# A cross-attention kernel: the half tile of keys moved to the seventh step of a group, two score buffers that alternate across groups, queries made in three stacked blocks

## What is computed

```
B = 16 batches, 256 queries of width 128, 1601 keys of width 96, 16 heads of width 64
xn  = layernorm(x)
sim = (xn Wq)(ctx Wk)^T / 8         per head, softmax over the 1601 keys
x   = x + softmax(sim)(ctx Wv) Wo + bo
h   = layernorm(x)
x   = x + experts(h) + shared(h)    32 experts, 4 chosen per token
```

## Time and profile before

| | |
|---|---|
| median of three executions | 3226.2 us |
| the profiled execution: its time, its span | 3223.51 us, 3221.7 us |
| PE matmuls busy | 3179.9 us, 99% |
| weight loads, DVE, ACT, POOL busy | 79%, 74%, 63%, 41% |
| mean granted clock of TensorE | 0.997 of 2.4 GHz |
| DMA, mean over the span | 21 GB/s |

### The profile page before, as it was taken

The page is one execution under the profiler, slowest core; times in us unless marked ns, Lnnn a source line. Parts: engine busy times, 40 slices in busy tenths (PEclk is TensorE's granted clock), DMA queues, the critical chain, the costliest instruction groups (busy, mean ns, idle before and its releaser), DMA issues.

```text
span 3221.7 us, 40836 instructions
## 1 busy us (share of the span) xinstructions
PE 3179.9 (99%) x15118; PEld 2534.7 (79%) x15118; DVE 2389.6 (74%) x4882; ACT 2017.8 (63%) x2356; POOL 1333.2 (41%) x894
## 2 busy tenths in 40 slices
PE   7999999999999999999999999999999999999999
PEld 5777777778777777778777777777877778777787
DVE  5777777777777777777777777777777777777766
ACT  4666666666666666666666666666666666676555
POOL 5333443334333343334443344333433334225566
PEclk8999999999999999999999999999999999999999
DMA  2000000000000000000000000000000000105553
GB/s 82 1 17 1 17 1 1 18 1 18 1 18 1 18 1 1 17 1 18 1 18 1 18 1 18 1 1 18 1 18 1 18 1 1 40 3 122 120 129 76
DMA packets 31707, 67.48 MB, mean 21 GB/s; under 512 B 8339, under 2 KB 9620, under 8 KB 31124
## 3 DMA queue, kind: packets, MB, share of 16 engines
q1 hardware_dynamic: 31508, 64.88, 7.8%
HBM read 61.72 MB, written 2.62 MB: 20 GB/s over the span
## 4 chain that ended last, share of the span: by engine, by line
PE 96%; DVE 1%; POOL 1%; issue 1%; ACT 0%; DMA 0%; POOLq 0%; SPq 0%; DVEq 0%; ACTq 0%
PE st L593 12%; PE st L596 12%; PE side L535 11%; PE op L606 11%; PE op L612 11%; PE st L599 11%; PE op L609 11%; PE side L629 3%; PE st L716 2%; PE st L718 2%; PE st L717 2%; PE side L528 1%; PE op L620 1%; PE op L623 1%; PE side L530 1%; PE side L529 1%
## 5 line engine op out<-in xcount | busy, mean ns | idle before, releaser
L473 POOL TENSOR_TENSOR p_lo<-p_full,p_hi 128x1024 fp32r<-128x1024 f32 x320 | 819.7, 2562 | 1753.1 <-ACT p_hi L877 1753.1
L1156 DVE TENSOR_REDUCE m_part<-side 128x1 f32<-128x400 f32 x2016 | 1072.7, 568 | 502.3 <-PE side L535 502.2
L874 ACT ACTIVATE p_full<-st 128x1024 f32<-128x1024 f32 x768 | 788.8, 1027 | 876.8 <-PE st L599 848.5
L877 ACT ACTIVATE p_hi<-st 128x1024 fp32r<-128x1024 f32 x768 | 784.9, 1022 | 0.0
L1139 DVE TENSOR_TENSOR p_lo<-p_full,p_hi 128x1024 fp32r<-128x1024 f32 x448 | 545.5, 1218 | 85.6 <-ACT p_hi L877 85.6
L535 PE MATMUL side<-cT_hi,qT_hi 96*128 96x400 f32 x2016 | 554.5, 346 | 0.0
L593 PE MATMUL st<-qT_hi,cT_hi 97*128 97x512 f32 x1664 | 540.8, 406 | 11.9 <-DMA qT_hi<-m_row 11.1
L596 PE MATMUL st<-qT_lo,cT_hi 96*128 96x512 f32 x1664 | 524.3, 396 | 0.0
L606 PE MATMUL op<-p_hi,v_hi 128*97 128x512 f32 x1536 | 487.6, 398 | 1.6 <-DVE p_lo L1139 1.6
L612 PE MATMUL op<-p_hi,v_lo 128*97 128x512 f32 x1536 | 480.4, 394 | 0.0
L609 PE MATMUL op<-p_lo,v_hi 128*97 128x512 f32 x1536 | 480.4, 394 | 0.0
(11 more groups left out here) (171 smaller groups left out, 3072.1 us busy)
## 6 DMA issues: line engine op xcount, KB each, us to landing
w_rep<-w_rows SPq DMA_DIRECT2D x64, 512.0 KB, 6.6
keys_nat<-in_ctx_keys SPq DMA_DIRECT2D x16, 672.0 KB, 6.0
keys_tur<-in_ctx_turned SPq DMA_DIRECT2D x16, 600.4 KB, 4.8
gud_raw<-in_moe_w SPq DMA_DIRECT2D x2, 1152.0 KB, 7.7
out_x<-x SPq DMA_DIRECT2D x8, 256.0 KB, 2.0
x<-in_x SPq DMA_DIRECT2D x1, 1920.0 KB, 12.7
qT_hi<-m_row SPq DMA_DIRECT2D x64, 4.0 KB
oT<-e_row SPq DMA_DIRECT2D x64, 4.0 KB
```

What stands on the lines that cost most here:

```text
L473: pool.tensor_tensor(p_lo[:, slot(s), :], p_full[:, s % 2, :], p_hi[:, slot(s), :].bitcast(F32), ALU.subtract).then_inc(s_lo_pool, 1)
L874: act.activation(p_full[0:m, s % 2, :], made, ACT.Exp, scale=SCALE)
L877: act.activation(p_hi[0:m, slot(s), :], made, ACT.Exp, scale=SCALE).then_inc(s_ex, 1)
L1156: dve.tensor_reduce(m_part[:, k % NT, k // NT:k // NT + 1], where[:, 0:MAXW], AX.X, ALU.max).then_inc(s_drain, 1)
```

## The change

1. The half tile is worked at step 6 (`HALF = 6`), the full tiles 6 to 11 at steps 7 to 12. `low_half` on ACT now stands ahead of the exponentials of step 6, `sum_half` on DVE at t = 6, and `scores(8)`, which reuses the buffer, waits for the sum. POOL still has steps 3, 5, 7, 9, 11.
2. A group has 13 steps, an odd number, so the buffers of scores and of `p_full` are taken by `(n + s) % 2` with n = 13 g: they alternate on across the end of a group. `scores(0)` of the next group waits for the exponentials of step 11, `scores(1)` for those of step 12.
3. The 4 x 96 columns of A of a group are stored as three blocks of 128. Queries are made with three times three matmuls of 128x256 instead of four times three of 96x256. The fourth head's queries come out in the rows 96 to 127 of the three blocks, and ACT and DVE move them to their place by pieces: the first job has three pieces (96x512 and two of 32x256), the second two (96x256, 32x256).
4. `PLACES`: one M goes from behind `weigh(4)` at t = 6 to behind `weigh(0)` at t = 2; of the two Q the first stands ahead of `weigh(10)`, the second behind it.
5. At the end of a group ACT does the exponentials of step 12 ahead of `queries_hi`, and DVE does `p_lo` of step 12, the query pieces, then both `early_steps` and `late_steps`.

```diff
-        PLACES = {2: ("MM", "M"), 3: ("MM", "M"), 4: ("MM", "MM"), 5: ("MM", "M"), 6: ("MM", "MM"),
+        PLACES = {2: ("MM", "MM"), 3: ("MM", "M"), 4: ("MM", "MM"), 5: ("MM", "M"), 6: ("MM", "M"),
                   7: ("MM", "MM"), 8: ("MM", "MY"), 9: ("MM", "MM"), 10: ("MM", "MM"), 11: ("YY", "YT"),
-                  12: ("QQ", "")}
+                  12: ("Q", "Q")}
...
+        def unstacked(tile, where, k):
+            last = slice(3 * NQ, GQ)
+            if k == 0:
+                return [(tile[0:DC, 0:BANK], where[0:DC, :]),
+                        (tile[0:DT, last], where[DC:P, 0:NQ]),
+                        (tile[DT:2 * DT, last], where[DC:P, NQ:BANK])]
+            return [(tile[0:DC, BANK:3 * NQ], where[0:DC, 0:NQ]),
+                    (tile[2 * DT:DC, last], where[DC:P, 0:NQ])]
...
-                for h in range(2):
-                    head = g * GH + 2 * k + h
-                    o = where[0:DC, h * NQ:(h + 1) * NQ]
-                    pe.matmul(o, A_hi[:, head, :], x_hi[:, half, :], start=True, stop=False)
+                for block in ((0, 1), (2,))[k]:
+                    o = where[:, block % 2 * NQ:(block % 2 + 1) * NQ]
+                    pe.matmul(o, A_hi[:, g, block, :], x_hi[:, half, :], start=True, stop=False)
...
                 def qk(s):
-                    pe.wait_ge(s_ex, n + (s - 1))
-                    scores(s, i % 2, par)
+                    if s - 2 == HALF:
+                        pe.wait_ge(s_sum, g + 1)
+                    else:
+                        pe.wait_ge(s_ex, n + (s - 1))
+                    scores(n, s, i % 2, par)
...
-                pe.wait_ge(s_sum, g + 1)
+                pe.wait_ge(s_ex, n + (S - 1))
                 if i == NGB - 1:
                     pe.wait_ge(s_v, NGB * (b + 2))
-                scores(0, (i + 1) % 2, next_par)
-                scores(1, (i + 1) % 2, next_par)
+                scores(n + S, 0, (i + 1) % 2, next_par)
+                pe.wait_ge(s_ex, n + S)
+                scores(n + S, 1, (i + 1) % 2, next_par)
                 pv(S - 1)
...
                 for t in range(2, S):
                     if t == S - 1:
+                        lo(t - 1)
+                        lo(t)
+                        side_jobs(at[t][0])
+                    elif t == HALF:
+                        side_jobs(at[t][0])
+                        lo(t - 1)
                         sum_half()
-                        side_jobs(at[t][0])
-                        early_steps()
-                        lo(t)
...
+                early_steps()
                 late_steps()
```

More of the change, by code:

```diff
@@ L587, in _, with scores @@
             turn_maxima(bank(J0_T))
-            def scores(s, slot, par):
-                keys = slice(s * P, s * P + P)
+            def scores(n, s, slot, par):
+                tile = tile_of(s)
+                keys = slice(tile * P, tile * P + P)
                 halves = [slice(j * BANK, (j + 1) * BANK) for j in range(2)]
+                into = st[:, (n + s) % 2]
                 for j in range(2):
-                    pe.matmul(st[:, s % 2, j, :], cT_hi[par][:, keys], qT_hi[slot][:, halves[j]],
-                              start=True, stop=False)
+                    pe.matmul(into[:, j, :], cT_hi[par][:, keys], qT_hi[slot][:, halves[j]], start=True, stop=False)
                 for j in range(2):
[L596 to L599, removed]
+                    mm = pe.matmul(into[:, j, :], cT_hi[par][0:DC, keys], qT_lo[slot][:, halves[j]],
+                                   start=False, stop=(s == HALF))
+                for j in range(0 if s == HALF else 2):
+                    mm = pe.matmul(into[:, j, :], cT_lo[par][:, keys], qT_hi[slot][0:DC, halves[j]],
                                    start=False, stop=True)
@@ L798, in queries_hi @@
                 act.wait_ge(s_fill, filled)
-                act.activation(qT_hi[slot][0:DC, k * BANK:(k + 1) * BANK], where[0:DC, :], ACT.Copy).then_inc(s_qh, 1)
+                for into, made in unstacked(qT_hi[slot], where, k):
+                    ins = act.activation(into, made, ACT.Copy)
+                ins.then_inc(s_qh, 1)
             def products(banks, cols):
                 return banks[:, :, cols].rearrange("p j (c m) -> p j c m", c=2)
-            def four_heads(tile, n):
-                return tile[:, 4 * n:4 * n + 4, :].rearrange("p (c j) m -> p j c m", c=2)
             def keep_products(n, banks):
@@ L809, in keep_products @@
                     act.wait_ge(s_ab, 2 * n + 2)
-                    act.activation(four_heads(A_raw, n), products(banks, slice(0, 2 * DC)), ACT.Copy)
-                    act.activation(four_heads(A_hi, n), products(banks, slice(0, 2 * DC)), ACT.Copy)
+                    for tile in (A_raw, A_hi):
+                        for into, made in stacked(tile, n, banks):
+                            act.activation(into, made, ACT.Copy)
                 b = B_all[0:DC, 4 * n:4 * n + 4, 0:D].rearrange("p (c j) m -> p j c m", c=2)
@@ L817, in _ @@
             act.wait_ge(s_ab, 2)
-            act.activation(four_heads(A_hi, 0), products(op, slice(0, 2 * DC)), ACT.Copy).then_inc(s_xh, 1)
+            for into, made in stacked(A_hi, 0, op):
+                ins = act.activation(into, made, ACT.Copy)
+            ins.then_inc(s_xh, 1)
             act.wait_ge(s_tur, 16)
@@ L880, in low_half @@
                 def low_half():
-                    act.wait_ge(s_qk, n + S)
-                    act.activation(s_half[:, :], both(st[TAIL:P, FULL % 2]), ACT.Copy).then_inc(s_low, 1)
+                    act.wait_ge(s_qk, n + HALF + 1)
+                    act.activation(s_half[:, :], both(st[TAIL:P, (n + HALF) % 2]), ACT.Copy).then_inc(s_low, 1)
                 exp(0)
@@ L887, in body @@
                     keep_output(n)
-                for s in range(1, FULL):
+                for s in range(1, S):
+                    if s == HALF:
+                        low_half()
                     exp(s)
@@ L1000, in queries_lo @@
                 dve.wait_ge(s_qh, count)
-                cols = slice(k * BANK, (k + 1) * BANK)
-                dve.tensor_tensor(qT_lo[slot][:, cols], where[0:DC, :], qT_hi[slot][0:DC, cols].bitcast(F32),
-                                  ALU.subtract).then_inc(s_drain, 1)
+                high = unstacked(qT_hi[slot], where, k)
+                for (into, made), (kept, _) in zip(unstacked(qT_lo[slot], where, k), high):
+                    ins = dve.tensor_tensor(into, made, kept.bitcast(F32), ALU.subtract)
+                ins.then_inc(s_drain, 1)
             def combine_max():
@@ L1100, in _ @@
             dve.wait_ge(s_xh, 2)
[L1101 to L1104 removed]
+            for (into, made), (kept, _) in zip(stacked(A_lo, 0, op), stacked(A_hi, 0, op)):
+                ins = dve.tensor_tensor(into, made, kept.bitcast(F32), ALU.subtract)
+            ins.then_inc(s_Al, 1)
             for k in range(2):
```

98 lines of the change are left out of this document (49 added, 49 removed).

## The result

| | before | after |
|---|---|---|
| median | 3225.82 us (5 runs, 3223.34 to 3226.91) | 3240.12 us (5 runs, 3239.82 to 3241.05) |
| ratio of the means, with its 95% interval | | 1.0046 (1.0031 to 1.006) |
| profiled execution: time, span | 3223.51, 3221.7 us | 3239.88, 3238.1 us |

The forecast was 3229.5 us, 3.7 above the median measured for before; measured are 14.3 above it. That is inside the range of 3206 to 3244, but 1.1 us above the 3239 that my own case had as its upper bound, and four times the predicted difference, and with 0.46% on the side of "slower by over 0.2%", to which I had given 0.29 and "within 0.2%" 0.36.

The account below looks back on a forecast made before the run. PE was taken as the bound, with matmuls in flight 99% of the span. Per group -0.35 - 0.18 + 0.31 + 0.17 + 0.13 = +0.08 us, times 62 = +5; start +1, end -2: +4 us, forecast 3229.5 us, range 3206 to 3244.

Parts of the forecast that it names:

- my own case: The forecast from the summed terms, three new waits on PE included: 3229.5 us, bounds 3221 to 3239, chance 0.50.
- Queries, -0.35 us a group: Nine query matmuls instead of twelve on PE, pace kept at 0.117 us: 0.35 us less a group, 21.8 us over 62.
- The wait ahead of them, -0.18: Before the query matmuls, PE's wait for DVE to empty Y's bank goes, behind a full tile's scores: 0.18 us a group.
- t = 3, +0.31: The second M of t = 3 waits for the bank of the M added at t = 2: 0.31 us more a group.
- t = 6, +0.17: Behind the half tile's shorter scores, the second M waits for its bank: 0.17 us mean, about 0.26 at i = 1, 2.
- t = 8, +0.13: Behind the half tile's shorter weigh(6), Y waits for the bank of the second M of a pair: 0.13 us a group.
- The end of a group, taken as 0: DVE's pieces and routing steps ahead of step 0's p_lo nearly hidden before weigh(0): 0 to 0.1 us in one group of four.
- the rule for side jobs: A side job on PE effectively starts 0.16 us after DVE has emptied its bank, or when due, whichever is later.
- Start, +1: Ahead of the first group, ACT and DVE move weights' products and queries in pieces: about 1 us more, once.
- End, -2: At the very end PE no longer stands 2.9 us for the half tile's chain; 0.7 us left, 2 us less.
- the slower rivals: DVE late at step 0 (3252 us, chance 0.12) and the wider query weights showing on PE (3243 us, chance 0.05).
- DVE is late at step 0: Query pieces taking 0.2 us more each on DVE hold weigh(0) at i = 1 and 2: 22 us, 3252 us, chance 0.12.

Follow-up runs that it names:

- before once more: The kernel before, unchanged, profiled again in one execution: 3226.55 us, beside 3225.94 us for before in its row; first T at 36.0 us.

## Why the prediction was right and where it was off

By its own steps, against before once more, which had no early clock either: the spans differ by 3238.1 - 3224.8 = 13.3 us, of which 2.4 lie ahead of the first T, -0.1 between it and the fifth, 11.3 from there to the last, -0.3 behind it.

- **Queries, -0.35 us a group: right** (0.35 to 0.36 by the run with the old queries). The pace kept its 0.12.
- **The wait ahead of them, -0.18: right.** In the trace above the second query matmul starts 0.12 behind the first (1128.87 - 1128.75), and so it does in the groups of every i. With i = 3, -0.35 - 0.18 + 0.31 + 0 + 0.23 gives +0.01, and +0.01 was measured. It was not tried alone.
- **t = 3, +0.31: right for i = 0, 1 and 3** (0.29 to 0.33). For i = 2 it was counted and did not show, since the wait at `weigh(0)` had already moved PE.
- **t = 6, +0.17: right** in size and by i: in the mean 0.15 with i = 0 (0.17 forecast), 0.25 with i = 1 and 2 (0.26) and, with i = 3, nothing.
- **t = 8, +0.13: the step that failed.** It costs 0.22 to 0.24 us in the groups of every i. I took the maxima at t = 7 at the distance from a low part that ordinary low parts have; the half tile's writes other rows and overlaps nothing, 0.11 us more, times 62 = 7 us. The rule of the Trainium skill that is named above stands in the prediction too, but for the query pieces alone, which I had already counted without overlap; I had not asked it of the half tile's low part.
- **The end of a group, taken as 0: the second step that failed.** It costs 0.29 us behind the groups of i = 1. In the rows above, with T at 1217.32, DVE ended step 0's low part 11.46 us behind T, not 11.2 (the pieces took 2.46 us, not 2.3, and the low part of step 12 came 0.1 later), and I did not add the 0.15 us of release that I had just made the rule for side jobs. In the sum it hides: it stands in for t = 3's wait at i = 2.
- **Start, +1: it was 2.4**; queries and products of more than one group are moved in pieces there, and I had counted about one set. **End, -2: it was -0.4.** The wait of 2.9 us for the half tile's chain did shrink, to 0.5 at `weigh(12)`. But the last group has no M that fills PE, and there PE now waits in its middle, for the half tile's low part at `weigh(6)` and for POOL at `weigh(7)`, which I had not looked at:

```profile
PE op L652 <- DVE p_hi L1170: 1.2, 1, 1.2
...
PE op L638 <- POOL p_lo L504: 0.6, 1, 0.6
```

- **The offset.** I set the forecast 2.7 us above my sum, because the trace of before lay under the median. That was right: its start-up ran at the higher clock. (3223.5 + 4 + 2.7 is 3230 and not 3229.5; the slip changes nothing.)

So the mechanisms of my case came true, and its size did not: 3240.1 lies above its 3221 to 3239, and inside 3206 to 3244 only by the room that was left for the slower rivals. That the end of a group, taken as 0, did no harm to the sum was luck, since the wait of t = 3 that it stands in for is about as long. Of the rivals, "DVE is late at step 0" was real in its mechanism, at 16 x 0.29 = 5 us where it had 22. By terms: t = 8 gives 6 to 7 us of the 9 to 10 that were missing, the start 1.4, the end 1.6; the rest is small.

## What to carry to other kernels

Where two queues run within 0.1 us of each other, a price per group must contain what lets an instruction overlap its neighbours, and for every wait the latency of its release; look at the first partition that each instruction writes. Where two waits follow each other on the engine that is the bound, take away both: at i = 2 either alone gave nothing and both gave 0.30 us, so an experiment that removes one shows nothing of its price. And a table of jobs that is the same for all groups pays for the heaviest of them: choosing it by i took 6.5 us here (3221.0 to 3214.5; 5.3 of it between the fifth and the last T), where the change itself took none.

## What the chip showed that I had not expected

- The same kernel starts at either clock: four matmuls of 400 columns took 1.00 us in one execution and 1.70 us in another, from 13.4 us on, and the first T came 5.4 us apart, of which 3.3 were left at the fifth. A profile of one execution is a draw, and here the forecast's reference was the one of fourteen traces that had it early.
- A VectorE instruction of 64 rows that writes rows 64 to 127 costs its neighbours 0.11 us on each side; with rows 0 to 63 as output, and the same inputs, nothing. Here that was worth 7.35 us of 3226.
- A wider weight load (128 instead of 96 columns) behind matmuls of 256 columns costs next to nothing: they start 0.119 instead of 0.118 us apart.
